# Routed tokens written to their expert slots by indirect row transfers

## What is computed

```
E, K = 8, 2;  cap = int(T / E * 1.25)                  # 80 slots per sequence and expert
probs = softmax(x @ Wr + br);  topk_p, topk_e = top_k(probs, K)
oh  = one_hot(e_flat, E);  pos = (cumsum(oh, 1) - oh) at e_flat   # place in the expert's queue
keep = pos < cap
flat_idx = (e_flat * B + b_idx) * cap + minimum(pos, cap - 1)
buf = zeros(E * B * cap, C).at[flat_idx].add(x_rep * keep)
h = relu(buf[e] @ W1[e] + b1[e]);  y = h @ W2[e] + b2[e]          # (640 x 256) @ (256 x 1024) @ (1024 x 256) per expert
y_tok = y[flat_idx] * (p_flat * keep);  out = sum over the two picks
```

## Time and profile before

| | us |
|---|---|
| median of three runs | 3171.58 (3170.65 to 3173.0) |
| the profiled execution | 3169.16 |
| its span, first to last instruction | 3167.4 |
| setup | 0 to 103 |
| passes (0, -, -) and (1, 0, -) | 103 to 370 |
| six passes of the loop | 370 to 1880 (about 252 each) |
| pass (-, 7, 6) | 1880 to 2090 |
| pass (-, -, 7) | 2090 to 2197 |
| experts | 2197 to 2496 (35.4 each after the first) |
| layer 2 | 2496 to 3167 |

### The profile page before, as it was taken

The page is one execution under the profiler, slowest core; times in us unless marked ns, Lnnn a source line. Parts: engine busy times, 40 slices in busy tenths (PEclk is TensorE's granted clock), DMA queues, the critical chain, the costliest instruction groups (busy, mean ns, idle before and its releaser), DMA issues. The chain is left out here.

```text
span 3167.4 us, 33541 instructions
## 1 busy us (share of the span) xinstructions
PE 2413.1 (76%) x11754; PEld 1587.2 (50%) x11754; DVE 1562.1 (49%) x3728; ACT 1037.9 (33%) x2567; POOL 830.2 (26%) x583
## 2 busy tenths in 40 slices
PE   6258877777777767877777777855999597979798
PEld 5134444444444444544444444533777357574747
DVE  2468567466565765745755754422000144444443
ACT  2024343343343334334234334321222151515050
POOL 0435243153153134225224321020000223232220
PEclk9567886877777677688688688677999797979787
DMA  3000100110020010010020010022222302020200
GB/s 144 35 15 1 55 21 1 42 43 1 10 75 1 9 58 18 9 56 21 1 64 21 1 55 21 1 69 82 90 90 90 103 1 65 3 59 9 56 12 14
DMA packets 66386, 120.48 MB, mean 38 GB/s; under 512 B 29621, under 2 KB 43947, under 8 KB 63795
## 3 DMA queue, kind: packets, MB, share of 16 engines
q1 hardware_dynamic: 53434, 76.51, 7.2%
q0 software_dynamic: 12800, 41.95, 4.8%
HBM read 97.36 MB, written 21.07 MB: 37 GB/s over the span
## 5 line engine op out<-in xcount | busy, mean ns | idle before, releaser
L1022 ACT ACTIVATE att_buf<-att_buf,nmin 128x384 f32<-128x384 f32 (+3 forms) x512 | 288.3, 563 | 854.2 <-DVE nmin L1344 854.0
L858 PE MATMUL bank<-kk,qT 32*128 32x512 f32 (+2 forms) x1024 | 352.7, 725 | 92.1 <-DVE nmin L1344 92.0
L690 POOL TENSOR_TENSOR big<-ex_at,kx 128x2048 f32<-128x2048 f32 x64 | 236.6, 3705 | 428.1 <-DVE xt_na L1131 354.3
L885 PE MATMUL bank<-ident,att_buf 128*128 128x128 f32 x1280 | 254.0, 339 | 22.3 <-ACT att_buf L1030 19.2
L639 POOL TENSOR_TENSOR big<-kx 128x1280 f32<-128x1280 f32 x64 | 162.7, 2570 | 311.1 <-ACT kx L957 303.2
L1131 DVE TENSOR_REDUCE xt_na<-big 128x64 f32<-128x1024 f32 x128 | 240.8, 1899 | 2.2 <-POOL big L690 1.6
L1333 DVE TENSOR_TENSOR att_buf<-bank,wdiag 128x128 f32<-128x128 f32 x384 | 93.0, 284 | 288.9 <-PE bank L863 286.2
L899 PE MATMUL bank<-att_buf,vp 128*32 128x128 f32 x2560 | 234.0, 323 | 0.0
L1030 ACT COPY att_buf<-bank 128x384 f32<-128x384 f32 (+3 forms) x512 | 208.8, 410 | 21.8 <-PE bank L899 17.3
L885 PEld LDWEIGHTS bank<-ident,att_buf 128*128 128x128 f32 x1280 | 187.2, 179 | 33.8 <-ACT att_buf L1022 23.1
L858 PEld LDWEIGHTS bank<-kk,qT 32*128 32x128 f32 x1024 | 117.4, 234 | 165.7 <-DVE nmin L1344 124.5
(11 more groups left out here) (333 smaller groups left out, 4525.1 us busy)
## 6 DMA issues: line engine op xcount, KB each, us to landing
ew<-in_eW SPq DMA_DIRECT2D x16, 1024.0 KB, 8.4
buf_d<-gac SPq DMA_DIRECT2D x16, 320.0 KB, 2.8
eb<-buf_d SPq DMA_DIRECT2D x8, 640.0 KB, 3.6
y_d<-yy SPq DMA_DIRECT2D x8, 640.0 KB, 10.7
xt_na<-in_xT SPq DMA_DIRECT2D x8, 512.0 KB, 3.6
nA<-in_xN SPq DMA_DIRECT2D x8, 512.0 KB, 4.4
x_d<-x SPq DMA_DIRECT2D x8, 512.0 KB, 4.2
kf<-x_d SPq DMA_DIRECT2D x8, 512.0 KB, 3.2
```

The source lines that it names most:

```text
L690: pool.tensor_tensor(pv[:, :, c * P:(c + 1) * P].rearrange("p o (h d) -> p o h d", d=DH), spread(ex[:, t, :, 8 * c:8 * c + 8], 3, DH), spr ...
L858: pe.matmul(bank[u % 2][:, 0:n], qT[r:r + 32, g, i * P:(i + 1) * P], kk[r:r + 32, g, T * i * P:T * i * P + n], start=True, stop=False)
L885: mm = pe.transpose(bank[3 + u % 2][:, j * P:(j + 1) * P], pr[:, u % NPR, j * P:(j + 1) * P], ident[:])
L1022: act.activation(pr[:, u % NPR, 0:n], pr[:, u % NPR, 0:n], ACT.Exp, scale=-1.0, bias=nmin[:, u % 4:u % 4 + 1], accum_out=rsum[:, i, h:h + ...
```

## The change

The expert inputs are kept as rows: `buf_d` becomes a table of 8 x 640 rows of 256 floats, followed by 1024 spare rows. In the setup SP writes zeros to the 5120 slot rows. In each pass DVE computes, for each token and pick, the row number (`gi[:, 2 + k]`, the same as in `y_d`) if the pick is kept, and a spare row of its own if not. GpSimd issues eight indirect row transfers (two picks x four token tiles, 128 rows of 1 KB each) from `nB` to `buf_d`, behind its products in program order, then waits for each and resets its semaphore. The one-hots, their matmuls, the copies to `bfT` and the two stores go. In the experts the rows are loaded as they are (`er`), and PE turns them in ten transposes of 128 x 128 (`turned`); DVE copies the result to `eb` in three copies (`rows_out`). The turning of expert k + 1 stands between the hidden layer and the outputs of expert k.

```diff
-    buf_d = nc.dram_tensor("buf_d", [E, P, K2, B, CAP], F32, kind=scratch_kind).ap()
+    buf_d = nc.dram_tensor("buf_d", [E * ROWS + 2 * S, D], F32, kind=scratch_kind).ap()
...
# setup, SP:
+        sp.wait_ge(s("zero_ok"), 1)
+        for e in range(E):
+            sp.dma_start(buf_d[e * ROWS:(e + 1) * ROWS].rearrange("(t p) d -> p t d", p=P), spread(zero[:], 1, ST))\
+                .then_inc(s("zeroed"), 16)
         sp.wait_ge(s("drow_ok"), 1)
...
+        sp.wait_ge(s("zeroed"), 16 * E)
...
# setup, GpSimd:
+        pool.memset(zero[:], 0.0).then_inc(s("zero_ok"), 1)
...
# pass, SP:
-            sp.wait_ge(s("gi_ok"), 1)
+            sp.wait_ge(s("sidx_ok"), 1)
             sp.dma_start(gate_d[b3], gi[:].rearrange("p k t -> p (k t)")).then_inc(s("out3"), 16)
-            for m in range(K2):
-                sp.wait_ge(s("bf_ok"), 2 * m + 2)
-                sp.dma_start(buf_d[:, :, m, b3, :].rearrange("e p c -> p e c"),
-                             bfT[:, m, :].rearrange("p (e c) -> p e c", c=CAP)).then_inc(s("out3"), 16)
...
# pass, GpSimd, at its end:
+        if b3 is not None:
+            pool.wait_ge(s("sidx_ok"), 1)
+            for k in range(2):
+                for t in range(T):
+                    pool.indirect_dma_start(
+                        out=buf_d, out_offset=bass.IndirectOffsetOnAxis(ap=sidx[:, k, t:t + 1].bitcast(U32), axis=0),
+                        in_=nB[:, t, :], in_offset=None).then_inc(s(f"scat{k}{t}"), 16)
+            for k in range(2):
+                for t in range(T):
+                    pool.wait_ge(s(f"scat{k}{t}"), 16)
+                    pool.dma_reset(range(s(f"scat{k}{t}").num, s(f"scat{k}{t}").num + 1))
...
# pass, PE, before the transposes at slot 55:
-                pe.wait_ge(s("bf_ok"), 4)
+                pe.wait_ge(s("pos_out"), 1)
...
# pass, PE, at slots 46 to 50:
-            w = SLOTS // 2
-            for m in range(K2):
-                for c in range(2):
-                    yield AT["disp"] + 3 * m + c
-                    pe.wait_ge(s("disp_ok"), T)
-                    if m:
-                        pe.wait_ge(s("bf_ok"), c + 1)
-                    for t in range(T):
-                        mm = pe.matmul(bank[SIDE[c]][:, 0:w], nB[:, t, m * P:(m + 1) * P],
-                                       disp[:, t, c * w:(c + 1) * w], start=(t == 0), stop=(t == T - 1))
-                    mm.then_inc(s("bf_mm"), 1)
...
# pass, ACT:
-            for n in range(4):
-                yield AT["disp"] + 3 * (n // 2) + n % 2 + 1
-                act.wait_ge(s("bf_mm"), n + 1)
-                act.copy(bfT[:, n // 2, (n % 2) * w:(n % 2 + 1) * w], bank[SIDE[n % 2]][:, 0:w]).then_inc(s("bf_ok"), 1)
...
# pass, DVE, for each pick k:
-                step(dve.tensor_scalar(slot, sm[:, 4 + k], float(CAP), 1.0, ALU.mult, ALU.add))
-                step(dve.tensor_tensor(slot, slot, at, ALU.add))
-                step(dve.tensor_tensor(slot, slot, keep, ALU.mult))
-                step(dve.tensor_scalar(slot, slot, -1.0, None, ALU.add))
...
# pass, DVE, after the picks:
-            for t in range(T):
-                yield AT["disp"] - T + t
-                step(dve.tensor_scalar(disp[:, t, :], iota[:], sm[:, 10, t:t + 1], None, ALU.is_equal))
-                dve.scalar_tensor_tensor(disp[:, t, :], iota[:], sm[:, 11, t:t + 1], disp[:, t, :],
-                                         ALU.is_equal, ALU.add).then_inc(s("disp_ok"), 1)
+            yield AT["pos"] + 5
+            row_of, keeps = gi[:, 2:4], sm[:, 8:10]
+            step(dve.tensor_tensor(sx[:, 0], row_of, spare[:], ALU.subtract))
+            step(dve.tensor_tensor(sx[:, 1], sx[:, 0], keeps, ALU.mult))
+            step(dve.tensor_tensor(sx[:, 2], sx[:, 1], spare[:], ALU.add))
+            dve.tensor_copy(sidx[:], sx[:, 2]).then_inc(s("sidx_ok"), 1)
...
# experts, SP:
-            for dst, src in ((eb[:, n].rearrange("p m r -> p (m r)"), buf_d[e].rearrange("p m b c -> p (m b c)")),
+            for dst, src in ((er[:, n], buf_d[e * ROWS:(e + 1) * ROWS].rearrange("(t p) d -> p t d", p=P)),
                              (eb1[:, n], a["eb1"][e]), (ew1[:, n], a["eW1"][e])):
...
# experts, PE:
+        def turned(k):
+            pe.wait_ge(s(f"w1_in{k % 2}"), 48 * (k // 2 + 1))
+            for t in range(ST):
+                for m in range(K2):
+                    dst = bank[m][:, t * P:(t + 1) * P] if t < 4 else bank[2][:, m * P:(m + 1) * P]
+                    mm = pe.transpose(dst, er[:, k % 2, t, m * P:(m + 1) * P], ident[:])
+            mm.then_inc(s("ebT_mm"), 1)
+
+        turned(0)
         for k in range(E):
-            pe.wait_ge(s(f"w1_in{k % 2}"), 48 * (k // 2 + 1))
+            pe.wait_ge(s("ebT_ok"), 3 * (k + 1))
...
             pe.wait_ge(s("h_ok"), 2 * KH * (k + 1))
+            if k + 1 < E:
+                turned(k + 1)
             pe.wait_ge(s(f"w2_in{k % 2}"), 32 * (k // 2 + 1))
...
# experts, DVE:
+        def rows_out(k):
+            dve.wait_ge(s("ebT_mm"), k + 1)
+            for m in range(K2):
+                dve.tensor_copy(eb[:, k % 2, m, 0:4 * P], bank[m][:]).then_inc(s("ebT_ok"), 1)
+            dve.tensor_copy(eb[:, k % 2, :, 4 * P:5 * P], bank[2][:, 0:2 * P].rearrange("p (m r) -> p m r", m=K2))\
+                .then_inc(s("ebT_ok"), 1)
+
+        rows_out(0)
         for k in range(E):
+            if k + 1 < E:
+                rows_out(k + 1)
```

More of the change, by code:

```diff
@@ L133, in program @@
                 identb = sb("identb", [P, P], BF16)
-                iota = sb("iota", [P, SLOTS])
+                iota = sb("iota", [P, E])
+                spare = sb("spare", [P, 2, T])
                 wdiag = sb("wdiag", [P, H, P])
```

28 lines of the change are left out of this document (14 added, 14 removed).

## The result

The changed kernel takes 3054.59 us (median of four runs, 3046.54 to 3062.34) against 3171.11 for the kernel before beside it: ratio 0.9636, 95% interval 0.9607 to 0.9665, 116.5 us less. The forecast was 71 less, with 3070 as its lower end: the direction was right, the size too small. Each trace is of one execution; this one took 3046.54 us, 8 under its median, and gained 122.6 on that of before.

| stage | before | after | difference | forecast |
|---|---|---|---|---|
| setup | 103.3 | 103.3 | 0 | 0 |
| passes (0, -, -), (1, 0, -) | 266.9 | 264.2 | -2.7 | 0 |
| six loop passes | 1509.6 | 1410.0 | -99.6 | -72 |
| pass (-, 7, 6) | 210.3 | 191.3 | -19.0 | -8 |
| pass (-, -, 7) | 106.7 | 99.8 | -6.9 | -5 |

The account below looks back on a forecast made before the run. No engine is full in a loop pass; lockstep pairs last as long as the longer of VectorE and TensorE. 3169.2 - 72 - 8 - 5 + 14 = 3098, with 2.4 for the median 3101 us, range 3070 to 3137.

Parts of the forecast that it names:

- The walk over the six pairs: Loop pass from slot 42: each lockstep pair lasts as long as its longer engine; 37.8 us falls to 23.1 or 29.2.
- So I take neither end: 12 us a pass: Loop passes: a gain chosen between 8.6 (half clock) and 14.7 (full clock), over six passes -72 us.
- "full clock" end: Six pairs of a loop pass with TensorE at full clock: 23.1 us, 14.7 less than 37.8.
- the lower end: Loop pass gain at half clock throughout: 8.6 us, or 6 if later pairs that are fast today also slow down.
- Rival C: Loop passes: the fast stretch also covers the conditioning output projection, 16 to 18 us a pass, 3065 to 3077; chance 0.12.
- rival A: Loop passes: the forecast itself, 10 to 14.7 us gained a pass, 3085 to 3113 us; chance 0.50.
- Rival B: Loop passes: clock stays at 1.2 GHz after slot 46 without L789, gaining 6 to 8.6 us a pass, 3121; chance 0.22.
- The pass (-, 7, 6): Pass after the loop: TensorE loses 9.7 to 13.5 us, partly beside VectorE waits; -8 taken between 0 and 13.5.
- The last pass: Routing end to first expert load: eight bare writes 10.05 us, then 6.89; -5, bounds -9 (landing takes 3) and +2.
- Experts: Ten transposes at 1.3 us for experts 2 to 8, 9.1, plus 5 before the first: +14, bounds +9 and +20.
- Setup and cover: Zero stores fit within the setup's 103 us; a loop pass's writes fill 17 of some 46 us GpSimd slack: cost 0.
- Rivals D and E: D: scatters cost GpSimd more than gathers, chance 0.07. E: zeros or row loads uncovered, 15 to 70 us, chance 0.09.

Follow-up runs that it names:

- late_projection: Changed kernel with a row-load semaphore and earlier turning, plus the conditioning output projection (L739) moved from slot 57 to slots 60 and 62; 3090.31 us.
- mm_back: Changed kernel with the 32 matmul instructions of each routed sequence put back on TensorE, without the one-hots; 3099.13 us, ratio 0.9777.
- scatter_twice: Changed kernel with every indirect write issued twice, the second eight of a pass after the first have landed; 3069.99 us, ratio 0.9673.
- both_back: Changed kernel with one-hots and their matmuls both put back, no copies or stores, indirect writes staying; 3176.91 us, ratio 1.003.
- hot_later: Changed kernel with VectorE's one-hots put back, read by nobody, at slots 48 to 51 beside the indirect writes; 3135.17 us, ratio 0.9909.
- the two tails: Changed kernel with row-load semaphore and earlier turning, VectorE's last instruction of each pass repeated two or four more times; 3078.2 and 3069.09 us.

## Why the prediction was off

- **The walk over the six pairs** was the right mechanism: lockstep, VectorE then TensorE, both pieces needed. It failed at "So I take neither end: 12 us a pass". Measured, 37.8 became 21.5, 16.3 less (21.7 in the second trace); the "full clock" end was 14.7. The first, third and fourth pair came as written (3.2, 3.5, 3.5 for 3.3, 3.7, 3.6). The mis-sized pair is the second, "still starts at half clock", 5.2: it took 3.7 with the rise in it, and 4.8 to 5.0 in passes without. A choice in the middle had nothing to stand on: the pairs take 20.7 us with the early rise and some 23.3 without.
- **The rest of the loop pass** held +2.9 from slot 54 on (L739's surroundings and L952 at half clock: the lower end had "later pairs slow down"), and -1.9, -0.6 and -0.7 ahead of the pairs. The -0.7 is the index steps. The -1.9 is within what two traces of one kernel differ by: the second trace of before has 41.8 there for 43.1. Rival C named the size by the first traces (16.6 a pass), but not the cause: L739's pair took 10.9 after 11.4. By the second traces of both kernels a loop pass gained 14.2, within rival A.
- **Rival B** is refuted for the change, since no L789 is needed for the rise. As a state of the clock it is real, for a pair or two at a time: in two of six passes of the changed kernel, in three of late_projection.
- **The pass (-, 7, 6)**, -8: the six pairs went from 31.5 to 18.4, -13.1. The matmuls alone cost 7.2 of that in mm_back, at a clock of 0.96, so as the price of the matmuls the 8 was about right. What the sum left out is the clock: 0.76 granted in the pairs of before, 0.95 after, and scatter_twice shows what the level is worth there (25.5 us at 0.57). 0.8 more are index steps, and 5.3 lie in slots 2 to 9 (17.7 to 12.4), which the change doesn't touch. both_back has the short ones too, and hot_later, late_projection and the two tails have long ones. The clock is down in them; what sets it for a given kernel stays open.
- **The last pass**, -5: eight writes took 9.97 us (10.05), and after them 3.0 us passed, not the 6.89 of sixteen gathers: the lower bound was the true one. Routing ended 0.8 later in the pass, so -6.9.
- **Experts**, +14: the seven turnings cost 1.05 each (1.3), 7.3. The first cost the 4.1 us of its turning, but the weights were there 6.9 after the first load where they had taken 9.1, so 1.9 net (5). Why they landed sooner was not tried.
- **Setup and cover**, 0: right. The setup ends at 103.25, GpSimd idles 36 us, and doubling the writes costs nothing in a loop pass. Rivals D and E had no part. (In rival D, 64 s at s = 5.5 is 352, not 354.)

The gain between the first traces, 122.6, is 51.6 above the forecast 71: 27.6 of it in the loop passes (13.2 by the second traces), 11.0 in the pass (-, 7, 6), 4.7 in the experts, 1.9 in the last pass, and 6.4 in stages that the change leaves alone. So the two steps that failed are both the clock's: the middle value for the six pairs of a loop pass, and a pass (-, 7, 6) priced without it. The last 6.4, and half of the loops' 27.6, are the luck of one trace.

## What to carry to other kernels

In a lockstep of two engines walk the pairs with each engine's work and believe the walk. Put removed pieces back one by one and together, and price them in the pairs where they stand: lengths of whole passes also hold what differs from trace to trace. A step whose clock can be either of two levels has two values, not a mean, and the same code can take either in two passes of one execution: trace each kernel twice, compare by stage over several passes, and don't tune by what a single pass gains. Work added to a full engine is cheapest in the idle time in front of a wait.

## What was not expected of the hardware

- The same pass code varied from 235.0 to 241.3 us within one execution. The six pairs differ by 2.6 us with the granted clock (0.50 or about 0.85 over the second and third), and the time before the first pair by 6.7, much of it from VectorE products that take 3 us beside GpSimd products and 0.96 without.
- TensorE without any idle time for 8.3 us stayed at 0.50 (late_projection). Most of that stretch is scores over 32 rows and transposes. With the same 150 instructions, six pairs took 25.5 us at 0.57 and 18.4 at 0.95.
- In three passes of late_projection TensorE, ScalarE and VectorE stood idle together for 3.3 us or more, with an end that the profile doesn't place on the core.
- VectorE compares of 128x640 took 0.58 us with GpSimd issuing transfers and up to 3.11 with a GpSimd product running; compare-and-adds 0.89 and up to 4.18. By the Trainium skill (SBUF - State Buffer, Who interferes with whom) VectorE's second port is GpSimd's, and one holds it for a whole instruction; the rows agree.
- Eight indirect writes of 128 rows of 1 KB cost GpSimd 1.28 us each and land within 3 us of the last.
